# Transforms folded twice in half of their frequencies, and loop bodies cut into pieces of up to four sequences

## What is computed

```python
def xattn(query, memory, Wq, bq, Wk, bk, Wv, bv):
    s = sigmoid(norm(query)); repeat 10 times: s = 3.9 * s * (1 - s)
    q = query * (1 + 0.1 * (s - 0.5)) * (1 + 0.1 * wave)
    Q, K, V = q @ Wq.T + bq, mem @ Wk.T + bk, mem @ Wv.T + bv
    Qf, Kf, Vf = fft(Q, axis=-2), fft(K, axis=-2), fft(V, axis=-2)
    QKV = hamilton(hamilton(Qf * filt, Kf * filt), Vf * filt)
    return ifft(QKV, axis=-2).real
def ffn(inputs):   # top-1 of 8 experts, capacity 1024 rows each
    tokens = layer_norm(inputs)
    top1 = argmax(tokens @ gate.T); rank = place among the rows of that expert
    return inputs + weight * expert_out[top1, slot]      # gelu(t @ wi) @ wo
x = x + xattn(layernorm(x), ctx, ...)
x = x + ffn(layernorm(x), ...)
```

## Time and profile before

| | us |
|---|---|
| median of 3 runs | 3754.94 (3754.02 to 3754.99) |
| the profiled execution, own time | 3758.4 |
| its span, first to last instruction | 3756.6 |
| first stage, up to the last scatter | about 2299 |
| PE, DVE, ACT, POOL busy | 3512.3, 2616.5, 1529.5, 1498.0 |

### The profile page before, as it was taken

One profiled execution on the slowest core, in us unless ns is written; L12 is line 12 of the kernel. 1 busy time (PEld: TensorE's weight loads), 2 busy tenths in 40 slices (PEclk: granted clock), 3 DMA queues, 4 the chain that ended last, 5 costly groups with the idle time before them and its releaser, 6 DMA issues. The chain is left out here.

```text
span 3756.6 us, 49624 instructions
## 1 busy us (share of the span) xinstructions
PE 3512.3 (93%) x15056; PEld 2638.9 (70%) x15056; DVE 2616.5 (70%) x4304; ACT 1529.5 (41%) x2598; POOL 1498.0 (40%) x2985
## 2 busy tenths in 40 slices
PE   6999989989989989989989986999999999999998
PEld 4666656656666666666666664888888888888886
DVE  5889788789788788788888884444444444444443
ACT  4434435435435435435435433333333333333332
POOL 5665665675665666666666641000000000000000
PEclk8999999999999999999999997999999999999999
DMA  5421211211211221211221213333333333333331
GB/s 178 168 86 57 85 51 56 79 57 56 79 52 49 79 68 45 93 65 45 79 68 45 68 35 113 112 101 124 113 114 123 113 124 113 107 107 103 122 101 45
DMA packets 223435, 327.03 MB, mean 87 GB/s; under 512 B 36832, under 2 KB 102624, under 8 KB 223232
## 3 DMA queue, kind: packets, MB, share of 16 engines
q1 hardware_dynamic: 207904, 307.97, 24.0%
q0 software_dynamic: 15360, 16.99, 1.3%
HBM read 256.82 MB, written 101.97 MB: 96 GB/s over the span
## 5 line engine op out<-in xcount | busy, mean ns | idle before, releaser
L1180 POOL TENSOR_TENSOR tally<-tally,unit 1x1 f32<-1x1 f32 x16 | 2.9, 180 | 1357.6 <-DVE mixed L1361 1357.6
L406 PE MATMUL pair<-w_q,q_spec 128*128 128x512 f32 x1024 | 460.5, 598 | 24.1 <-ACT q_spec L576 24.1
L1288 ACT ACTIVATE act<-hid_ps 128x512 f32<-128x512 f32 x256 | 153.1, 598 | 802.4 <-PE hid_ps L1219 802.4
L1349 DVE CAST act_h<-act 128x512 fp32r<-128x512 f32 x256 | 109.4, 427 | 527.9 <-ACT act L1288 527.9
L1219 PE MATMUL hid_ps<-tok_h,w_h 128*128 128x512 f32 x1024 | 405.6, 396 | 3.8 <-DVE tok_l L1337 2.3
L1219 PE MATMUL hid_ps<-tok_l,w_h 128*128 128x512 f32 x1024 | 399.7, 390 | 0.0
L1219 PE MATMUL hid_ps<-tok_h,w_l 128*128 128x512 f32 x1024 | 399.1, 390 | 0.0
L1235 PE MATMUL out_ps<-w_l,act_h 128*128 128x512 f32 x1024 | 398.6, 389 | 0.0
L1233 PE MATMUL out_ps<-w_h,act_h 128*128 128x512 f32 x1024 | 398.3, 389 | 0.0
L1234 PE MATMUL out_ps<-w_h,act_l 128*128 128x512 f32 x1024 | 398.3, 389 | 0.0
L1343 DVE TENSOR_TENSOR w_l<-w_raw,w_h 128x2048 fp32r<-128x2048 f32 x128 | 293.4, 2293 | 90.8 <-ACT w_h L1282 90.8
(11 more groups left out here) (177 smaller groups left out, 8469.2 us busy)
## 6 DMA issues: line engine op xcount, KB each, us to landing
w_raw<-in_L_ffn_wi SPq DMA_DIRECT2D x128, 512.0 KB, 3.5
w_raw<-in_L_ffn_wo SPq DMA_DIRECT2D x128, 512.0 KB, 4.7
w_raw<-in_x SPq DMA_DIRECT2D x32, 1024.0 KB, 5.2
w_raw<-in_ctx SPq DMA_DIRECT2D x32, 1024.0 KB, 7.1
x_res<-in_x SPq DMA_DIRECT2D x31, 1024.0 KB, 5.3
out<-x_res SPq DMA_DIRECT2D x31, 1024.0 KB, 4.3
slots<-rows SPq DMA_DIRECT2D x4, 4160.0 KB, 20.7
got<-slots SPq DMA_DIRECT2D x16, 1040.0 KB, 7.2
```

The source lines that it names most:

```text
L406: last = nc.tensor.matmul(pair[k % 2][:, s, :], spec[:, c, tile * 256 + s * P:tile * 256 + (s + 1) * P], w[:, c, :], start=(c == 0 and n = ...
L1288: nc.scalar.activation(act32[i % 2][:], hid_ps[i % 2][:], ACT.Gelu).then_inc(gelu, 1)
L1349: v.tensor_copy(act_h[i % 4][:], act32[i % 2][:]).then_inc(ah_ready, 1)
```

## The change

It has three parts, all in the first stage.

1. The even frequencies get a second fold. Of the 256 frequencies, the 128 even ones need only the sum of rows n and n + 256; now that sum is folded again (rows n and n + 128), and the multiples of 4 take its sum, the others its difference. A unit of `dft` has two products of 128 columns in place of two of 256, and the two for the odd frequencies stay. DVE writes the first sum in place in the loaded rows and has two more instructions of 512 elements in each of `folds_q` and `folds_c`. The matrices `fwd_e`, `fwd_o` replace `fwd`; the inverse's rows are put in the same order.
2. `products` does its 8 multiplications of 512 elements as 2 of 2048, with one operand repeated by a step of zero; `sums` reads the blocks from their new places.
3. Every engine's loop body is written as a list of small pieces for sequences from b - 4 to b, with `on(b)` leaving out those beyond the ends. DVE and PE loop over 22 bodies from 7 to 28, ACT and POOL over 24 from 6 to 29, SP over 23, and the bodies before and behind are written out (14 of DVE and PE, where it was 6). `inverse` and `add_attended` are split in two, the copies of the real bins are apart from `real_parts` (with a semaphore `real_ev` of their own, by which `convert` of the even half now starts), and `squares_x2`, `sums_x` are no longer mixed with the spectra.

```diff
+                        even = ps[:, 0:256].rearrange("p (s h j) -> p h s j", s=2, h=2)
+                        for h in range(2):
+                            nc.tensor.matmul(even[:, h], folded[:, 0, h, u * P:(u + 1) * P], fwd_e[:, h],
+                                             start=True, stop=True)
+                        for t in range(2):
+                            last = nc.tensor.matmul(ps[:, 256:512], folded[:, 1, t, u * P:(u + 1) * P], fwd_o[:, t],
+                                                    start=(t == 0), stop=(t == 1))
...
-                        for eo, op in ((0, ALU.add), (1, ALU.subtract)):
-                            v.tensor_tensor(dst[:, eo], src[:, 0:2], src[:, 2:4], op).then_inc(ready, 1)
+                        v.tensor_tensor(dst[:, 1], src[:, 0:2], src[:, 2:4], ALU.subtract).then_inc(ready, 1)
+                        v.tensor_tensor(src[:, 0:2], src[:, 0:2], src[:, 2:4], ALU.add).then_inc(ready, 1)
+
+                    def fold_again(b, src, dst, ready):
+                        dve.wait_ge(ready, b * FOLD + 2)
+                        v.tensor_tensor(dst[:, 0, 0], src[:, 0], src[:, 1], ALU.add).then_inc(ready, 1)
+                        v.tensor_tensor(dst[:, 0, 1], src[:, 0], src[:, 1], ALU.subtract).then_inc(ready, 1)
...
-                        for m, (i, j) in enumerate(((0, 0), (1, 1), (0, 1), (1, 0))):
-                            o = prod[:, m].rearrange("p w (h l e) -> p w h l e", h=2, l=2)
-
-                            hc.step(v.tensor_tensor(o[:, 0], view(l, i, 0, (3, 0)), view(r, j, 0, (2, 1)), ALU.mult))
-
-                            hc.step(v.tensor_tensor(o[:, 1], view(l, i, 1, (1, 0)), view(r, j, 2, (-2, 1)), ALU.mult))
+                        every = prod[:].rearrange("p (s m) w n -> p s (m w n)", s=2)
+                        lead, row = l[:, 0, 0:1, :], r[:, 0, 0:1, :]
+                        left = bass.AP(lead.tensor, lead.offset, [list(lead.ap[0]), [4 * P, 2], [P, 4], [0, 2], [1, P]])
+                        same = bass.AP(row.tensor, row.offset, [list(row.ap[0]), [4 * P, 2], [0, 2], [1, 4 * P]])
+                        other = bass.AP(row.tensor, row.offset + 4 * P, [list(row.ap[0]), [-4 * P, 2], [0, 2], [1, 4 * P]])
+                        hc.step(v.tensor_tensor(every[:, 0], left, same, ALU.mult))
+                        hc.step(v.tensor_tensor(every[:, 1], left, other, ALU.mult))
```

More of the change, by code:

```diff
@@ new lines, in project @@
+                        for c in range(CB):
+                            for n, (spec, w) in enumerate(terms):
+                                last = nc.tensor.matmul(pair[k % 2][:, s, :],
+                                                        spec[:, c, tile * 256 + s * P:tile * 256 + (s + 1) * P],
+                                                        w[:, c, :], start=(c == 0 and n == 0),
+                                                        stop=(c == CB - 1 and n == len(terms) - 1))
@@ L525, in _ @@
+                    for b in range(7):
+                        body(b, b % 2)
+                    with pe.Fori(7, 29, 2) as b:
+                        body(b, 1)
+                        body(b + 1, 0)
+                    for b in range(29, BATCH + 4):
+                        body(b, b % 2)
                 @block.scalar
@@ L697, in _ @@
+                    for b in range(6):
+                        body(b, b % 2)
+                    with act.Fori(6, 30, 2) as b:
+                        body(b, 0)
+                        body(b + 1, 1)
+                    for b in range(30, BATCH + 3):
+                        body(b, b % 2)
                 @block.gpsimd
@@ L844, in _, with body @@
-                    for b, p in ((BATCH - 2, 0), (BATCH - 1, 1)):
-                        mean2(b)
-                        stats2(b, p)
-                        scatter(b, p)
+                        if on(b):
+                            mean_of(s2c, b, sums2, sum2, neg2)
+                    def body(b, p):
+                        mean1(b)
+                        stats2(b - 3, 1 - p)
+                        stats1(b)
+                        scatter(b - 3, 1 - p)
+                        real_bins(b - 1)
+                        mean2(b - 2)
@@ L849, in _ @@
+                    for b in range(6):
+                        body(b, b % 2)
+                    with pool.Fori(6, 30, 2) as b:
+                        body(b, 0)
+                        body(b + 1, 1)
+                    for b in range(30, BATCH + 3):
+                        body(b, b % 2)
                 @block.vector
@@ L1078, in xattn_moe_kernel @@
+                    for b in range(7):
+                        body(b, b % 2)
+                    with dve.Fori(7, 29, 2) as b:
+                        body(b, 1)
+                        body(b + 1, 0)
+                    for b in range(29, BATCH + 4):
+                        body(b, b % 2)
         experts(nc, outer, slots, eye, gam, bet, w_raw, raw_in, wi, wo, out)
```

779 lines of the change are left out of this document (398 added, 381 removed).

## The result

| | before | after |
|---|---|---|
| median | 3754.97 us | 3619.10 us |
| runs | 3754.02 to 3757.57 | 3615.81 to 3623.75 |
| profiled execution, its span | 3758.4, 3756.6 us | 3623.75, 3621.9 us |
| one body (slot numbers 0 to 29, by 29) | 69.78 us | 64.86 us |

The ratio is 0.9638 [0.9621, 0.9655]: 136 us less, where 115 were forecast. The profiled execution was the longest of the four after the change.

A forecast was written before the change was run, and what follows sets the result against it. TensorE and VectorE take turns being late in 69.78 us bodies, with GpSimd's speed depending on VectorE. Body 65.8: 3758.4 - 119 (30 bodies) + 4 (start) = 3643, less 3.5 for the median: 3640 us; own range 3600 to 3675, 8-in-10 range 3548 to 3745.

The forecast's parts named there:

- the likeliest case: A ring through GpSimd sets the body's end and VectorE idles some 3.4 us: body 64.5 to 66.9 us, chance 0.48.
- the layout: VectorE's 25 steps and GpSimd's beside them, timed from `products(b - 2, 1)`; one body ends at 64.5 us.
- The additions to it: On the laid-out 64.5 us: 0.8 for small GpSimd operations slowing VectorE, 0.5 for the loop's branch; body 65.8 us.
- +4: Start: four ScalarE passes over the weights come behind the spectra of sequence 0, between 0 and +8 us; tail nothing.
- The price of the short products: TensorE's 128-column instructions at 0.118 us, where long ones cost 0.216: a body saves 3.1 us.
- The low clock: TensorE's lower clock level, 1.2 GHz, after idling; 1.8 us a body was expected to go, leaving its queue 59.6 us.
- What the change adds without writing it down: `products` offers GpSimd 8 instruction ends a body, not 32; a small operation meeting one waits up to 2.2 us.
- Rival A: GpSimd never sets the pace and VectorE is the bound: body 63.0 us, 3555 us, chance 0.22.
- B: `mean2` misses its gate by one or two long products: body 67.5 to 69.3 us, about 3705 us, chance 0.15.
- C: GpSimd falls four instruction ends behind and `convert(5)` is held 4.5 us: body 71.4 us, 3808 us, chance 0.12.
- D: Port held both ways, so VectorE waits out six GpSimd powers, 5.6 us: body 71.4 us, 3808 us, chance 0.03.
- E: TensorE's short products cost as much as long ones or more: body 65.8 to 67 us, no chance of its own.

The follow-up runs named there:

- `products(5)` in pieces: Changed kernel with only the last product, `products(b - 2, 5)`, as eight multiplications of 512 and the others merged: 3727.81 us, ratio 0.9928.
- the map on ScalarE and VectorE written out: Changed kernel with `products(5)` as eight instructions, the scale map of `stats1` moved from GpSimd to ScalarE, VectorE's 22 looped bodies as straight-line code: 3503.54 us.
- all products in pieces: Changed kernel with each two multiplications of 2048 as eight of 512 again, order and folds kept: 3609.56 us, ratio 0.9610.
- nine operations fewer: `stats1` with 37 and not 46 GpSimd operations, same result: 3663.78 us on the changed kernel with `products(5)` as eight instructions, 3615.41 us on the changed kernel.
- three ways of shortening the wait: Changed kernel with all products as eight multiplications, 3609.56 us; with `base_of` behind `real_bin(b - 1, 0)`, 3683.16 us; with only `products(5)` as eight, 3727.81 us.
- The order alone: Changed kernel with the merged products and the second fold both undone, leaving the new order: 3603.97 us, ratio 0.9593.

## Why the prediction was right

The time lay in the range and the likeliest case was the one that came. That it came was in part luck: the case hung on `mean2` ending before `products(4)`, which the layout gave 0.2 us, and it came with 0.73 us in one body and level in the next. By its steps:

- **The layout.** It held along the whole body. Forecast and measured, in us from `products(b - 2, 1)`: `mean2` done 35.3 and 35.5; `products(4)` starts 35.5 and 36.2; `mean1` 43.6 and 43.8; `stats2` done 55.45 and 55.9; `convert(b - 1, 0)` starts 60.5 and 60.8, after a wait of 3.4 and 3.27; the next `products` 64.5 and 64.93. GpSimd's `stats1` and scatters ended at 12.1 for 14.7 and at 21.2 for 23.9, and in the body before, at 14.6 and 23.5, as laid out. The next bodies are equally long, so that cost nothing.
- **The additions to it.** +0.8 for small operations that hold VectorE up, and +0.5 for the branch. The laid-out points came 0.4 late at the end, so the first was half of what was booked. The branch cost nothing that shows: VectorE has no stall there in any round, and bodies alternate by 0.2 us (64.95, 64.75), while the looped kernels with two folds and `products(5)` in pieces stand 2 to 5 us at it. That the wait at `convert(b - 1, 0)` covers it is likely and not shown, as those stalls came behind waits too. The body is 64.86 and not 65.8: 30 x 0.94 = 28 us of the miss.
- **Start and end.** +4 was booked; -134.7 + 30 x 4.92 = +12.9 came. VectorE's first product stands at 68.74 us and not at 62.88, which fits the +0 to 8 of the weights; the rest, which lies in the deeper order's filling and draining, was not priced. It is 9 us of miss the other way: 3643 - 28 + 9 = 3624, the profiled execution's own time.
- **TensorE.** The price of the short products was right, four in 0.45 us, 0.11 each and not 0.216:

```profile
1178.23 0.61 PE L434 MATMUL xt_ps<-fwd_e,c_fold 128*128 128x128 f32 x4
1178.68 1.03 PE L437 MATMUL xt_ps<-fwd_o,c_fold 128*128 128x256 f32 x4
...
1214.70 0.74 PE L510 MATMUL xt_ps<-eye,rows 128*128 128x128 f32 x4 [1.81 <-ACT x_tok_t L687]
1215.23 1.17 PE L434 MATMUL xt_ps<-fwd_e,c_fold 128*128 128x128 f32 x4
1216.19 1.91 PE L437 MATMUL xt_ps<-fwd_o,c_fold 128*128 128x256 f32 x4
```

  The low clock did not go, though: behind the wait of 1.81 us for ScalarE the same eight took 1.17 and 1.91 us for 0.61 and 1.03, at a granted clock of 0.56 from 1214.70 to 1218.10 us, so mostly at the lower level, and TensorE was busy 0.964 x 64.86 = 62.5 us a body, where 59.6 were forecast. In the kernel with the map on ScalarE and VectorE written out, whose TensorE hardly waits, it is 0.983 x 61.5 = 60.5 us. It cost nothing here, as VectorE waits in this stretch for `real_row` alone, behind `base_of`, which waits for GpSimd.
- **What the merge is worth.** -1.9 us a body on VectorE was booked among the gains. As work it came, 1.5 us of it (VectorE is busy 0.934 x 64.86 = 60.6 us a body merged and 0.958 x 64.77 = 62.0 in pieces), and was of no use as time: VectorE was not the pace, and what it held up was. Taking it back gave 10 us, not a loss.
- **"What the change adds without writing it down"**, the GpSimd that gets 8 instruction ends and not 32, was the right thing to look for, and was under-rated: with one fold and the map on GpSimd it costs 69 us in the old order and 90 in the new.
- **Rival A** (GpSimd never paces, 63.0 us): excluded by the wait, and its case came, with 61.5 to 61.7 us for its 63, once GpSimd was relieved. **B and C** hang on `mean2` passing its gate. It passed with 0.73 us to spare in one body and with nothing in the next, and two edits that looked like pure gains lost it. So their chances of 0.15 and 0.12 were not too high. (B's own bodies of 67.5 to 69.3 us give 3691 to 3745 us, so its "about 3705" stands in the lower half.) **D** (the port held both ways): of the two products beside the power of 3.13 us above, the second started while the power was under way and took 2.29 us like the first. The Trainium skill ("SBUF — State Buffer", § SBUF: two separate sides) has the lock in both directions; no run here shows VectorE held for the whole of a GpSimd operation. It loses a little: in the kernel before, the 512-long product beside which `real_bins` began took 0.88 us for the usual 0.68, and the three behind it 0.73. **E**: the short products cost half.
- **Straight-line code at no cost**: right. With 36 bodies of VectorE written out its trace shows no stall of over 0.5 us at the issue of an instruction in the first stage.

What failed came behind the prediction: the expectation that the stall at `convert(b - 1, 0)` is 3.3 us to be had. What stays open: the exact debt that GpSimd may carry into a body before `mean2` misses its gate (nine operations fewer were too few and 24 enough; nothing between was run), and what sets the length of the stall at VectorE's branch.

## To carry over

When an engine waits in every body, ask what its pause gives the others before taking it away: here it was the time in which GpSimd caught up, and of three ways of shortening the wait one gained 10 us and two lost 64 and 109. Price a merged instruction by what it holds up beside it, not only by its own time; and try the parts of a change apart and in both surroundings, since the second fold was worth about nothing (-6), 75 and 92 us depending on who set the pace. Follow a ring over as many bodies as it spans, with each engine's debt at the seam.

## What the runs showed of the hardware

- A small GpSimd operation of 0.20 us takes 1.9 to 2.4 us beside a VectorE instruction of 2048 elements with two SBUF inputs, and 1.06 beside one of 1024. A scatter's issue took 0.98 us where no VectorE instruction of over 512 elements ran, and 2.56 beside two of 2048, both in the body above:

```profile
1183.30 2.56 POOL L854 DMA_INDIRECT slots<-rows,slot_i  x1 [0.56 <-issue]
...
1190.60 0.98 POOL L854 DMA_INDIRECT slots<-rows,slot_i  x1 [0.30 <-issue]
```

- At the branch of VectorE's loop, with two bodies in it, the next instruction stood 1.7 to 2.0 us in every round of the kernel before, 2.7 to 3.8 in most rounds with the map relieved, up to 5.4 in the kernel with all products in pieces, and not at all in the changed kernel. Waits some instructions ahead don't always cover it: with only `products(5)` in pieces 3.7 us came behind waits of 5.4 and 2.2. Writing the 22 bodies out took 31.9 us off.
- A chain of dependent ScalarE operations on 128x4 runs at 0.33 us each (nine in 2.94), with a VectorE product of 2048 beside it for most of that time. A chain of dependent small operations on GpSimd runs at 0.28 us each when no long VectorE instruction is beside it.
- Two kernels can have the same body and a different bound. The order alone has 64.8 us by TensorE (99% busy) and the changed kernel 64.9 by the ring through GpSimd. Relieving GpSimd (the map on ScalarE, `products(5)` in pieces) and writing VectorE out brought 116 us to the second; the first, with the other products merged besides, gained 8.
